# A vision tower block on one core: copies by DMA instead of selection matmuls, and paired row maxima

## The reference

```python
# mixer, per image
q, k, v = proj(Wq), proj(Wk), proj(Wv)
ew = exp(w_bias * local_mask); ek = exp(k)
y  = sigmoid(q) * (ew @ (ek * v)) / (ew @ ek)
h  = layernorm(y @ out_w + out_b + flatten(x)) * ln_g + ln_b
# attention over 257 tokens (class token last here), 16 heads of 16
h  = h + holo_attention(layernorm(h))   # q, k, v, out each: (x @ basis.T) @ (amp * cos(phase)).T
# experts: 8 routed (top 2) and a shared one
```

## Time and profile before

| | |
|---|---|
| median of 3 runs | 2958.11 us (2955.83 to 2960.87) |
| the profiled execution | 2954.87 us, its span 2953.0 us |
| mean granted TensorE clock | 0.916 of full speed |
| busy in the span | PE 88%, DVE 61%, ACT 38%, POOL 21% |
| stage A | up to about 1610 us |

### The profile page before, as it was taken

The page is one execution under the profiler, slowest core; times in us unless marked ns, Lnnn a source line. Parts: engine busy times, 40 slices in busy tenths (PEclk is TensorE's granted clock), DMA queues, the critical chain, the costliest instruction groups (busy, mean ns, idle before and its releaser), DMA issues. The chain is left out here.

```text
span 2953.0 us, 57443 instructions
## 1 busy us (share of the span) xinstructions
PE 2595.7 (88%) x16871; PEld 2124.6 (72%) x16872; DVE 1788.6 (61%) x4711; ACT 1124.9 (38%) x2993; POOL 626.0 (21%) x581
## 2 busy tenths in 40 slices
PE   2689999999999999999996557499999899999999
PEld 2467777777776776767763446377777699999999
DVE  6466767777667777767761787733333345555555
ACT  0135444445454454444452211044444423333332
POOL 1212212112122121121101675500000022222222
PEclk9589999999999999999996555599999999999999
DMA  2000000000000000000000443222222211122211
GB/s 75 8 8 23 20 16 20 23 16 20 17 23 20 16 20 19 20 20 16 16 9 14 160 131 116 93 82 83 84 85 84 78 54 57 57 64 62 59 57 54
DMA packets 88092, 140.13 MB, mean 47 GB/s; under 512 B 13986, under 2 KB 59860, under 8 KB 87764
## 3 DMA queue, kind: packets, MB, share of 16 engines
q1 hardware_dynamic: 74836, 101.99, 11.5%
q0 software_dynamic: 13056, 35.67, 3.7%
HBM read 83.04 MB, written 54.03 MB: 46 GB/s over the span
## 5 line engine op out<-in xcount | busy, mean ns | idle before, releaser
L735 DVE TENSOR_REDUCE mx<-ps 128x1 f32<-128x257 f32 x1024 | 394.5, 416 | 238.4 <-PE ps L385 214.6
L582 ACT ACTIVATE pT<-ps 128x257 f32<-128x257 f32 x1024 | 343.2, 382 | 285.1 <-PE ps L402 283.8
L385 PE MATMUL ps<-km,q 128*128 128x258 f32 x1024 | 351.3, 360 | 46.8 <-DVE mx L735 23.9
L402 PE MATMUL ps<-q,km 128*128 128x258 f32 x1024 | 283.6, 304 | 2.1 <-ACT pT L582 2.1
L385 PEld LDWEIGHTS ps<-km,q 128*128 128x128 f32 x1024 | 197.4, 193 | 118.5 <-DVE mx L735 57.2
L928 POOL TENSOR_TENSOR rs<-rs,mhalf 128x2 f32<-128x2 f32 x32 | 22.5, 703 | 1004.3 <-DVE rs L687 1004.3
L402 PEld LDWEIGHTS ps<-q,km 128*128 128x128 f32 x1024 | 192.5, 193 | 46.6 <-issue 28.7
L1564 PE MATMUL ps<-zhi,whi 128*128 128x256 f32 x1056 | 214.2, 284 | 1.5 <-DVE zlo L1632 1.5
L1564 PE MATMUL ps<-zhi,wlo 128*128 128x256 f32 x1056 | 211.1, 281 | 0.0
L1564 PE MATMUL ps<-zlo,whi 128*128 128x256 f32 x1056 | 210.6, 281 | 0.0
L1694 POOL TENSOR_TENSOR mark<-rowid 128x1 f32<-128x1 f32 x33 | 6.5, 197 | 860.4 <-DVE idx L1650 860.4
(11 more groups left out here) (321 smaller groups left out, 6278.8 us busy)
## 6 DMA issues: line engine op xcount, KB each, us to landing
z<-zs SPq DMA_DIRECT2D x140, 128.0 KB, 2.0
ys<-z SPq DMA_DIRECT2D x140, 128.0 KB, 1.9
hb<-hscr SPq DMA_DIRECT2D x66, 256.0 KB
xs<-in_x SPq DMA_DIRECT2D x64, 256.0 KB, 3.9
hscr<-h SPq DMA_DIRECT2D x34, 256.0 KB, 2.1
out<-acc SPq DMA_DIRECT2D x32, 256.0 KB
uu<-in_wu SPq DMA_DIRECT2D x6, 768.0 KB, 5.3
raw<-in_wu SPq DMA_DIRECT2D x6, 768.0 KB, 4.9
```

The source lines that it names most:

```text
L385: pe.matmul(ps[:, n % 2, 0:NP], q2[p % 2][:, h // 2, t * P:(t + 1) * P], km[p % 2][:, h // 2, h % 2, :], start=True, stop=True).then_inc(m ...
L402: pe.matmul(o, km[p % 2][:, h // 2, h % 2, t * P:(t + 1) * P], q2[p % 2][:, h // 2, :], start=True, stop=True).then_inc(s_ps, 1)
L582: act.activation(pT[:, n // LT, n % LT, :], ps[:, 4 + n % 2, 0:N], ACT.Exp, scale=HD ** -0.5).then_inc(s_ok, 1)
L735: dve.tensor_reduce(mx[:, t, h:h + 1], ps[:, n % 2, 0:N], AX_X, ALU.max, negate=True).then_inc(mx_ok, 1)
```

## The change

- `stack`, `take_stack`, `sel` and bank 6's use go. SP copies the split q and k with DMAs inside SBUF: 6 DMAs for q (`spread_q`) and 6 for each half of k (`spread_k`) per image. The columns of `Wz` are put in another order for that, and `q2` gets four buffers.
- `scores` has three banks (4, 5, 6) instead of two.
- `maxima` works in pairs: two matmuls into banks 0 and 1, one reduce of 2 x 257 columns, 16 per image. The next pair waits for the reduce of the one before.
- `cls_tiles` is split over places 14 and 15. `cls_shift` goes from DVE to POOL (`cls_keys`). The exponentials are split (ACT, POOL, two small DMAs), so that the class key enters `values` in a single fp32r pass.
- The last projection (`attend_out`) is a single fp32r pass; ACT and DVE (`out_low`) make the parts.
- `mixer_norm` and `attn_norm` go from DVE to ACT (scale and bias), and POOL makes the bias: two more small operations each (`nb`, `nb2`).
- `MX_AT` and `VALUES_AT` are new. Fills of `km` go from DVE to POOL, several fills go.

The diff, cut to its core:

```diff
-    VALUES_AT = (9, 12, 14)
-    MX_AT = [3, 3, 3, 2, 3, 3, 3, 2, 2, 2, 2, 2, 2, 0, 0, 0]
+    VALUES_AT = (6, 9, 12)
+    MX_AT = [2, 2, 1, 2, 2, 1, 0, 0, 0, 1, 2, 1, 2, 0, 0, 0]
@@ sync
+        def spread_q(j, p):
+            sp.wait_ge(lo_ok, 2 * j + 2)
+            for part, places in zip((qhi, qlo), PLACES[0]):
+                for place in places:
+                    for k in range(2):
+                        sp.dma_start(q2[...], part[...]).then_inc(q_in, 16)
+        def spread_k(j, p, f):
+            if not isinstance(j, int) or j >= 2:
+                sp.wait_ge(s_ps, SN * (j - 2) + SN // FT * (f + 1))
...
         def step(b, p):
...
+            if has(b + 1):
+                spread_k(b + 1, p + 1, 1)
+            if has(b + 2):
+                spread_q(b + 2, p + 2)
...
+            if has(b + 2):
+                spread_k(b + 2, p + 2, 0)
             if has(b + 1):
                 sp.wait_ge(negm_ok, b + 2)
...
+                sp.wait_ge(pch_ok, b + 2)
+                sp.dma_start(pcs[...]).then_inc(pcs_in, 16)
+                sp.wait_ge(pcl_ok, b + 2)
+                sp.dma_start(pcs[...]).then_inc(pcs_in, 16)
@@ tensor
-        def stack(j, p, r):
...
+        def maxima(m, p, i):
+            g, t = i // LT, i % LT
...
+            pe.wait_ge(mx_ok, m * MXN + i + 2)
+            for k in range(2):
+                last = pe.matmul(ps[:, k, 0:NP], q2[...], km[...], start=True, stop=True)
+            last.then_inc(mx_ps, 1)
@@ scores
-            if n >= 2 or later(b):
-                pe.wait_ge(s_ok, b * SN + n - 1)
+            if n >= 3:
+                pe.wait_ge(s_ok, b * SN + n - 2)
+            elif later(b):
+                pe.wait_ge(s_ok, b * SN)
@@ scalar
-        def take_stack(j, p, r):
...
+        def mixer_norm(b, p):
+            act.wait_ge(p1, b + 1)
...
+            for t in range(LT):
+                act.activation(hres[p % U][:, t, :], ps[:, 3, t * D:(t + 1) * D], ACT.Identity, bias=nb[:, t:t + 1],
+                               scale=rs[:, t:t + 1]).then_inc(hn_ok, 1)
+        def attn_norm(b, p):
...
                     if n == 15:
                         act.wait_ge(pcr_ok, b + 2)
...
+                        act.activation(pce[:, 0:N], pcr[(p + 1) % 2][:], ACT.Exp, scale=HD ** -0.5).then_inc(pce_ok, 1)
+                        act.wait_ge(pce_ok, b + 2)
+                        act.activation(pcs[(p + 1) % 2][0:HD, :], pce[:], ACT.Copy).then_inc(pch_ok, 1)
@@ vector
+        def out_low(b):
+            dve.wait_ge(roh_ok, b + 1)
+            dve.tensor_tensor(ro[HARM:2 * HARM, :], ps[HARM:2 * HARM, 7, 0:L], ro[HARM:2 * HARM, :], ALU.subtract)
+        def maxima(m, i):
+            dve.wait_ge(mx_ps, m * MXN + i + 3)
+            dve.tensor_reduce(mx[:, t, 2 * QAT[g]:2 * QAT[g] + 2], ps[:, 0:2, 0:N], AX_X, ALU.max, negate=True)
@@ gpsimd
             pool.wait_ge(ln1, b * 5 + 5)
+            pool.tensor_tensor(nb[:], mv[:, :, 0], mneg[:], ALU.mult).then_inc(root1, 1)
+            pool.tensor_tensor(rs[:], rs[:], mhalf[:], ALU.pow).then_inc(root1, 1)
+            pool.tensor_tensor(nb[:], nb[:], rs[:], ALU.mult).then_inc(p1, 1)
...
+        def cls_keys(m, p):
+            pool.wait_ge(negm_ok, m + 1)
+            pool.tensor_tensor(pcr[p % 2][:], pcr[p % 2][:], negr[p % 2][0:NH, 0:N], ALU.add).then_inc(pcr_ok, 1)
+            pool.wait_ge(pch_ok, m + 1)
+            pool.tensor_tensor(pcl[:], pce[:], pcs[p % 2][0:HD, :], ALU.subtract).then_inc(pcl_ok, 1)
```

More of the change, by code:

```diff
@@ L328, in resonances @@
             for f in range(FT):
-                last = pe.matmul(ps[0:3 * HARM, 3, 0:N], basT[:, f, :], zT[:, f, :], start=(f == 0), stop=(f == FT - 1))
+                last = pe.matmul(ps[0:3 * HARM, 3, 0:L], basT[:, f, :], zT[:, f, 0:L], start=(f == 0), stop=(f == FT - 1))
             last.then_inc(r_ps, 1)
@@ L340, in heads_qk @@
             for f in range(FT):
-                last = pe.matmul(ps[:, 2 + f, 0:N], Wz[:, n, f * P:(f + 1) * P], rT[:], start=True, stop=True)
+                last = pe.matmul(ps[:, 2 + f, 0:NP], Wz[:, n, f * P:(f + 1) * P], rT[:], start=True, stop=True)
             last.then_inc(qk_ps, 1)
@@ L364, in cls_tiles @@
[L364 removed]
+        def cls_tiles(m, p, n):
+            pe.wait_ge(lo_ok, 2 * m + 2)
             if later(m):
                 pe.wait_ge(negm_ok, m)
[L368 to L373 removed]
@@ L486, in step @@
                     heads_qk(b + 2, 0)
-                if n < LAG and has(b + 1):
-                    stack(b + 1, p + 1, RN - LAG + n)
-                if n > LAG and has(b + 2):
-                    stack(b + 2, p + 2, n - LAG)
-                if len(todo) > 2:
-                    maxima(b + 1, p + 1, todo[2])
+                if len(todo) > 1:
+                    maxima(b + 1, p + 1, todo[1])
                 if has(b - 1):
@@ L546, in _ @@
         for f in range(FT):
-            last = pe.matmul(ps[96:P, 6, 0:B], basoT[:, f, :], onT[:, f, 0:B], start=(f == 0), stop=(f == FT - 1))
+            last = pe.matmul(ps[0:3 * HARM, 6, 0:B], basoT[:, f, :], onT[:, f, 0:B], start=(f == 0), stop=(f == FT - 1))
         last.then_inc(ro_ps, 1)
@@ L550, in _ @@
         pe.wait_ge(h2_ok, B)
[L551 removed]
+        pe.matmul(ps[:, 7, 0:D], ro[:, 0:P], wos[:], start=True, stop=True).then_inc(o_ps, 1)
     @block.scalar
@@ L588, in take_group @@
             act.activation(og[:, g, :], ps[:, 7, 0:N], ACT.Copy).then_inc(og_ok, 1)
+        def mixer_norm(b, p):
+            act.wait_ge(p1, b + 1)
+            if not isinstance(b, int) or b >= U:
+                act.wait_ge(h2_ok, b - U + 1)
+            for t in range(LT):
+                act.activation(hres[p % U][:, t, :], ps[:, 3, t * D:(t + 1) * D], ACT.Identity, bias=nb[:, t:t + 1],
+                               scale=rs[:, t:t + 1]).then_inc(hn_ok, 1)
+        def attn_norm(b, p):
+            act.wait_ge(p2, b + 1)
+            for t in range(LT):
+                last = act.activation(z[:, t, :], hres[p % U][:, t, :], ACT.Identity, bias=nb2[:, t:t + 1],
+                                      scale=rs2[:, t:t + 1])
+            last.then_inc(z_ok, 1)
         def step(b, p):
             for n in range(NH):
+                if n == 0 and has(b + 2):
+                    attn_norm(b + 2, p + 2)
                 if has(b):
```

347 lines of the change are left out of this document (175 added, 172 removed).

## The result

The changed kernel takes 3114.96 us (median of 4 runs, 3107.71 to 3146.85) beside 2957.15 for the kernel before: a ratio of 1.0552, 95% interval 1.0478 to 1.0627. The direction and the place of the loss were as forecast, the size was not: 158 us where 68 were predicted, 5 us beyond the range. The profiled execution took 3119.56 us, its span 3117.7, at a mean granted clock of 0.867. Ratios leave out executions more than 1.5% above the fastest of their kernel, which concerns one of four with the early input load, one of four with single maxima, late clso and normalisations on VectorE, and three of four with single maxima alone, whose ratio is of just these three.

The account below looks back on a forecast made before the run. TensorE's bulk work and the mixer's chain were taken to bound stage A in turns. Per step 0.35 + 1.0 (port) + 1.7 (clock) = 3.05 us, times 29 = +88, edges -20: 3023 us profiled, 3026 median; range 2900 to 3110.

Parts of the forecast that it names:

- sum to output: Stretch from first `mixer_sum` to first `mixer_out`: 8.56 us before, 8.3 predicted, a gain of 0.25.
- statistics to place 0: From the statistics' start to TensorE's start at place 0: 8.3 us before, 9.7 predicted, 1.4 more.
- place 0 to 5: Stretch between TensorE's starts at places 0 and 5: 15.12 us before, +1.2 predicted from waits on pairs.
- place 5 to sum: Stretch from place 5 to the next `mixer_sum`: 7.43 us before, 5.7 predicted, a gain of 1.75.
- TensorE's saving turns into waits: Per step: 6.7 us less TensorE work (stacking 3.84, class product 2.0, last projection 0.8) becomes waits; four stretches net +0.35.
- Rival 1: TensorE stays the bound, so the kernel gets faster: 2741 us, 2838 if half shows; chance 0.15.
- Chain at place 0: Mixer's statistics, ScalarE normalisations and class work, with the pair waiting for `pcr`, delay place 0: 9.7 us instead of 8.3.
- The clso copy: VectorE's small copy meets GpSimd's input split through the shared port, on the path through place 3: +1.0 us per step.
- The clock: TensorE's idle 3 us before place 0 halve its clock for 6 us behind: +1.7 us per step, bounds 0 and 7.5.
- Rival 3: Clock stays low for half of each step: +7.5 us a step, 3152 us; chance 0.15.
- The waits at places 0 to 5: Second pairs wait for first ones: about 0.65 us later at place 3, about 0.55 at place 4; +1.2 us.
- The edges: Setup fills -7, contended normalisations moved to ScalarE -5, last steps without mixer -8: together -20 us.

Follow-up runs that it names:

- the fastest version: Changed kernel with single maxima, clso copied at place 5, normalisations on VectorE, and 16 unread matmuls at place 15 before the wait for place 0: 2938.72 us, 0.9912.
- the repaired version: Changed kernel with single maxima, clso copied at place 5 and both normalisations back on VectorE, no unread matmuls: 3007.44 us, 1.0110.

## Why the prediction was right about the sign and wrong about the size

Its sum was 43.87 + 3.05 = 46.9 us for the step; the step at 930 us has 51.26. By its own stretches:

| stretch | predicted | this step | mean of 15 |
|---|---|---|---|
| sum to output | 8.3 | 8.36 | 8.35 |
| output to statistics | 4.2 | 4.22 | 4.56 |
| statistics to place 0 | 9.7 | 10.17 | 10.45 |
| place 0 to 5, with 1.0 for the port and 1.7 for the clock | 19.0 | 22.52 | 22.07 |
| place 5 to sum | 5.7 | 5.99 | 6.02 |

- **TensorE's saving turns into waits**: right. The single passes do what was claimed (the class product is one matmul of 0.44 us, L463 in the rows above, where two took 0.63 from start to start), and no wait for the DMA copies shows. Rival 1 needed 37 to 40 us per step; even the fastest version has 46.2, and 42.1 in its steps at full clock.
- **Chain at place 0**: right in mechanism (the wait is ended by `pcr`), 0.5 to 0.75 us short, since I priced ScalarE's normalisation by the exponential `ek` of equal shape, 385 instead of 562 ns. Taking both normalisations back gained 66 us.
- **The clso copy**: I took +1.0, having bounded it by 0 and 2.9. It met the split's second part in this step: 2.29 us, +2.1; in the mean 1.44, +1.3.
- **The clock**: the step of the prediction that failed. I priced one pause per step at 1.7 us, with 6 us at the half level behind it. There were about 11 us at the half level per step in the mean, behind two pauses, not one: I had found the wait at place 3 ("It comes about 0.65 later than before") without asking whether it would be long enough to lower the clock; it was 3.73 us. Rival 3 had this mechanism with 7.5 us, at 0.15. The trace has one step in which neither wait nor copy was long (place 0 at 990.53): clso took 0.20 us, the wait at place 3 was 1.65 us, the clock was low for 3.4 us of the stretch from place 0 to 5, and that took 18.4 us instead of 22.5, with 10.2 us low. Of the 4.1 us, 2.1 are the copy; the other 2.0 go with 6.8 us less at the half level, 0.3 us for each. A fit over the 26 steps of the trace, with the copy's time as the second term, gives the same. By this I estimate the clock at 3 us in the stretch, where 1.7 stood.
- **The waits at places 0 to 5**: less 1.0 us for its own low clock, that step is still 1.1 us above the 16.3 that I had without port and clock (15.12 + 1.2). The +1.2 was too low by as much; which wait it is was not tested.
- **Rival 3's price**: 3152 leaves out the 0.35 us of the chain and the 1.0 of the port; with them it is 3191. The measured 3115 lies between the forecast and that.
- **That the terms add up**: wrong in kind. I treated port, clock and chain as costs to be summed. The late clso copy freed 2.1 us and gave 10 us instead of some 60; the unread matmuls added 1.9 us and took 56 or 69 away. In these runs the falls of the clock moved with the waits: with one pause gone, more of them came at another.
- **The edges**: -20 predicted; -14 ahead of the first root and -3.6 behind the last.
- **The step before**: the prediction cut a clean one of 43.87; the mean is 45.50. It too has its disturbed steps: at each round of the hardware loop TensorE stands still, and the low clock follows.

```profile
952.99 0.38 PE L385 MATMUL ps<-km,q 128*128 128x258 f32 x1 [2.23 <-issue]
```

The run with less work in the kernel before went from a clock of 0.98 to 0.94 and was 52 us slower. The Trainium skill's page "TensorE: Matmul & The Clock Gate", section "What's actually happening", has the low state as the default, which activity releases; this run agrees with it, and the prediction had let that rule price one pause only.

What stays open: why the low stretch lasts 23 us in one piece with the late clso copy and 3 to 7 us in 39 of the changed kernel's 45, and why the same wait of 0.7 us lowers the clock in one step and not in the next. The changed kernel has no step at full clock, so its division between clock and waits is the estimate above. Three of its steps, of 54.6 to 57.4 us, had over 20 us at the half level, much of it behind place 5.

## What to carry to other kernels

Before work is taken off an engine that is busy 96% of the time, ask what it will stand still for, and read from the trace what a pause of that length did to its clock: here 1.9 us less work per step made the kernel 1.8% slower, and 16 useless matmuls in a pause made another version 2.0% faster. Don't look at the longest pause alone: once it was filled, the falls came at waits of 0.7 us. Compare the steps of one execution with each other, since those at full clock show what the order of work takes by itself. Price a saving with the waits that it uncovers, and expect the first repair to give little until the clock stays up. And when a DMA's issue moves in a queue, follow it to the GpSimd work it starts and to what VectorE does then: one moved load gained 1.6% in one version and cost 1.4% in another.

## What the runs showed of the hardware that I had not expected

- The granted clock was 1.00 during pauses of 2.2 and 3.7 us and fell to 0.50 only behind them, while TensorE was already busy again. In the pause of 2.75 us of the earlier trace rows it fell before the pause was over.
- It also fell at waits of 0.6 to 0.8 us with no longer one near: 24 of 48 falls in the repaired version, 25 of 31 with the pause filled; and 3 times, with less work in the kernel before, with no wait over 0.2 us just before. In the kernel before itself 33 waits of 0.7 to 0.8 us had no fall.
- Among equal steps of one execution, each us at the half level made a step 0.40 us longer (42.14 us at 1.00, 51.15 at 0.77).
- With shorter waits it could stay low for longer: 0.84 in 300:1500 with the 3.7-us pause gone, 0.89 with it.
- ScalarE's scale and bias by partition took 562 (from PSUM) and 586 ns (from SBUF) for 128x256, an exponential of the same shape 385; VectorE's subtract and multiply 535 and 406.
- A VectorE copy of four columns took 2.29 us beside a GpSimd operation of 2.85 and ended with it; 160 ns otherwise. `z` went from 406 ns to a mean of 1586 in the same way.
- Some 50 MB more of SBUF-to-SBUF DMA, a share of 0.24 instead of 0.07 in stage A, cost no time that can be measured: 1.0552 [1.0478, 1.0627] with them, 1.0522 [1.0496, 1.0549] with tiny ones.
